# Reordering the local-attention stage of a two-branch block across tiles, with q's two rotary products split around ScalarE's square

## What is computed

```python
h = shift_token(x)                       # upper 64 channels come from the token before
q, k, v = split(h @ wqkv)                # 8 heads of 64
q, k = l2norm(q) * qs, l2norm(k) * ksc
q, k = rotary_xpos(q, k)                 # q * cos + rotate_half(q) * sin, the same for k
# windows of 64 queries see their own and the previous window of 64 keys
attn = softmax(mask(q @ k.T * 8)); o = attn @ v
x = x + o @ wo
h = layernorm(shift_token(x)); a, g = split(h @ w1 + b1)
x = x + (a * gelu(g)) @ w2 + b2
```

## Time and profile before

| | |
|---|---|
| median of 3 runs | 907.86 us |
| the profiled execution: its time, its span | 909.96 us, 908.2 us |
| PE busy | 800.1 us (88%) |
| DVE busy | 664.4 us (73%) |
| ACT busy | 654.3 us (72%) |
| POOL busy | 523.9 us (58%) |
| granted PE clock, mean | 0.972 of full |
| chain that ended last, by engine | PE 56%, ACT 17%, DVE 16%, issue 7% |

### The profile page before, as it was taken

How to read it: one execution, slowest core, us unless ns; L and a number is a source line. 1 busy time by engine, 2 the same in 40 slices (tenths; PEclk the granted TensorE clock), 3 DMA queues, 4 the chain that set the end, 5 groups by cost and what they waited for, 6 DMA issues and landing times.

```text
span 908.2 us, 26049 instructions
## 1 busy us (share of the span) xinstructions
PE 800.1 (88%) x9848; PEld 610.5 (67%) x9848; DVE 664.4 (73%) x1347; ACT 654.3 (72%) x2053; POOL 523.9 (58%) x521
## 2 busy tenths in 40 slices
PE   4779999779999999999989887999999999988985
PEld 1458778557777778777756545777877777775652
DVE  1577998677887787877457767778787788745765
ACT  2337777479899899889743337989988998974463
POOL 0363333078888888888511017888888888951100
PEclk8899999889999999999999998999999999999997
DMA  9110001012222222222201121222222222222001
GB/s 308 44 45 3 4 4 41 3 47 55 57 57 63 55 58 55 60 57 63 51 18 24 29 63 37 64 53 58 57 61 56 62 52 58 58 51 100 1 36 58
DMA packets 64704, 48.24 MB, mean 53 GB/s; under 512 B 40410, under 2 KB 50948, under 8 KB 64068
## 3 DMA queue, kind: packets, MB, share of 16 engines
q1 hardware_dynamic: 64580, 46.57, 19.9%
HBM read 10.63 MB, written 2.10 MB: 14 GB/s over the span
## 4 chain that ended last, share of the span: by engine, by line
PE 56%; ACT 17%; DVE 16%; issue 7%; POOL 1%; DMA 1%; SPq 1%; DVEq 0%; ACTq 0%; POOLq 0%
PE ps L415 47%; PE ps L425 9%; ACT prob L880 6%; DVE nmax L1130 3%; ACT sq L822 3%; DVE nt L1158 2%; ACT V L849 2%; ACT oT L831 2%; DVE split L970 2%; ACT kT L856 1%; ACT pT L826 1%; DVE prob L1217 1%; DVE split L968 1%; DMA awo<-in_awo 1%; ACT qT L841 1%
## 5 line engine op out<-in xcount | busy, mean ns | idle before, releaser
L880 ACT ACTIVATE prob<-ps,nmax 128x128 f32<-128x128 f32 x512 | 181.8, 374 | 36.7 <-DVE nmax L1130 36.7
L415 PE MATMUL ps<-wqkv,split 128*128 128x512 f32 x576 | 188.2, 438 | 14.2 <-DVE split L970 10.1
L1348 POOL TENSOR_TENSOR prob<-prob,rinv 128x512 f32<-128x512 f32 x128 | 133.9, 1046 | 88.4 <-DVE rinv L1116 45.8
L415 PEld LDWEIGHTS ps<-wqkv,split 128*128 128x128 f32 x576 | 97.5, 195 | 33.5 <-DVE split L970 10.2
L1130 DVE TENSOR_REDUCE nmax<-ps 128x4 f32<-128x512 f32 x128 | 83.6, 686 | 48.3 <-PE ps L415 48.3
L425 PE MATMUL ps<-ident,prob 128*128 128x128 f32 x640 | 98.3, 276 | 13.9 <-POOL prob L1348 13.1
L880 ACT ACTIVATION_READ_ACCUMULATOR prob<-ps,nmax 128x1 f32 x512 | 109.0, 213 | 0.0
L1359 POOL TENSOR_TENSOR qr<-qr,ss 128x512 f32<-128x512 f32 x64 | 66.9, 1046 | 53.7 <-DVE qr L1142 53.7
L425 PEld LDWEIGHTS ps<-ident,prob 128*128 128x128 f32 x640 | 76.2, 142 | 28.3 <-POOL prob L1348 17.4
L415 PE MATMUL ps<-oT,wo 128*128 128x128 f32 x512 | 73.9, 287 | 22.0 <-ACT oT L831 22.0
L826 ACT ACTIVATE pT<-ps 128x512 f32<-128x512 f32 x128 | 80.0, 625 | 10.7 <-PE ps L425 9.1
(11 more groups left out here) (139 smaller groups left out, 1871.9 us busy)
## 6 DMA issues: line engine op xcount, KB each, us to landing
VB<-V SPq DMA_DIRECT2D x129, 128.0 KB, 2.4
kT<-kT SPq DMA_DIRECT2D x65, 128.0 KB, 2.4
XS<-X SPq DMA_DIRECT2D x32, 128.0 KB, 2.3
XS<-X SPq DMA_DIRECT2D x128, 32.0 KB, 1.9
D<-in_xT SPq DMA_DIRECT2D x8, 256.0 KB, 4.4
XS<-in_xT SPq DMA_DIRECT2D x2, 1024.0 KB, 6.7
out_T<-XS SPq DMA_DIRECT2D x8, 256.0 KB, 2.0
raw<-in_wqkv SPq DMA_DIRECT2D x2, 768.0 KB, 4.4
```

The source lines that it names most:

```text
L415: return nc.tensor.matmul(o, l, r, start=start, stop=stop, skip_group_check=True)
L880: nc.scalar.activation(prob[:, par, grp, s * P:(s + 1) * P], ps[:, 4 + grp, s * P:(s + 1) * P], ACT.Exp, bias=nmax[:, par, grp * 4 + s:grp ...
L1348: g.tensor_tensor(p4, p4, rinv[:, slot, 4 * grp:4 * grp + 4].unsqueeze(2).broadcast_to([P, 4, P]), ALU.mult).then_inc(l_prob, 1)
```

## The change

The programs of all engines in the local stage are rewritten, with the same arithmetic but for these:

- The scaling of q by its norm on POOL (L1359) goes. The scores are now those of an unscaled q. DVE takes raw maxima (`rawmax`) and multiplies them by the norm in a small product (`scaled_maxima`), and ACT's exponentials get the norm as `scale`, read from `ss` for each partition, beside the `bias` that they had.
- The split of the input moves from DVE to POOL, in pieces of one tile (`input_high`, `input_low`).
- The copy of v moves from ACT to DVE (`v_copied`), and `V` and `ss` get a third buffer.
- For q, DVE makes the sine products first, ACT squares after them, and DVE makes the cosine product after the square.
- Semaphores that counted two groups or both q and k become one for each.
- The steps of a tile are spread over more steps n: q is projected 3 ahead (before 2), and the values of tile n-2 (before n-1) come right behind the scores of tile n and the transposes of q of tile n+1.

The new order on PE, on DVE and on ACT, as the diff has it, and SP's step:

```diff
+                def local(n, par):                    # PE
+                    q_projected(n + 3)
+                    k_turned(n)
+                    k_projected(n + 2)
+                    probs_turned(n - 2, 1)
+                    scores(n)
+                    q_turned(n + 1)
+                    values_summed(n - 2)
+                    probs_turned(n - 1, 0)
+                    output(n - 3)
+                    v_projected(n)
...
+                def values_summed(m):
+                    if 0 <= m < TILES:
...
+                        wait(pe, l_oe, base + m)
+                        pe.wait_ge(l_pTe[0], base + m + 1)
+                        pe.wait_ge(l_pTe[1], base + m + 1)
+                        pe.wait_ge(l_ve, base + m + 1)
+                        pe.wait_ge(v_prev[m % 2], 32 * ((base + m) // 2 + 1))
...
+                def local(n, par):                    # ACT
+                    q_squared(n + 3)
+                    norm_floor(n + 2)
+                    q_copied(n + 1)
+                    norm_log(n + 2)
+                    exponentials(n, 1)
+                    norm_inverse(n + 2)
+                    probs_copied(n - 1, 0)
+                    exponentials(n, 0)
+                    k_copied(n + 1)
+                    k_squared(n + 3)
+                    o_copied(n - 2)
+                    probs_copied(n - 1, 1)
...
+                    k_scaled(n + 1)                   # DVE
+                    q_rotated(n + 2)
+                    q_summed(n + 2)
+                    q_sin(n + 3)
+                    inverse_sums(n - 1, 0)
+                    v_copied(n - 1)
+                    k_summed(n + 2)
+                    maxima(n, 1)
+                    scaled_maxima(n, 1)
+                    inverse_sums(n - 1, 1)
+                    maxima(n, 0)
+                    q_cos(n + 3)
+                    scaled_maxima(n, 0)
+                    added_to_x(n - 3)
...
+                    normalised(n, 0)                  # POOL
+                    input_low(n + 5)
+                    input_high(n + 6)
+                    k_rotated(n + 2)
+                    normalised(n, 1)
+                    k_cos(n + 3)
+                    k_sin(n + 3)
```

```diff
                 def back(n, par):                     # SP
-                    nxt = 1 - par
-                    copied = held(xs_before_local(L) + 32 * (n - 2))
-                    if live(n, -3, TILES):
-                        sp.wait_ge(xs_dma, copied)
+                    nxt, done = 1 - par, base + n + 1
+                    if live(n, -5, TILES):
+                        sp.wait_ge(xs_dma, xs_before_local(L) + 32 * (n - 4))
                     if live(n, 0, TILES):
-                        sp.wait_ge(l_tre, turned)
-                        wait(sp, l_score, scored)
+                        sp.wait_ge(l_tk, done)
+                        wait(sp, l_score[1], done - 1)
                         sp.dma_start(kT[:, nxt, :, 0:WIN], kT[:, par, :, P:P + WIN]).then_inc(k_prev[nxt], 16)
                         sp.wait_ge(l_ve, done)
-                        sp.dma_start(VB[64:P, par, :], V[0:64, par, :]).then_inc(v_prev[par], 16)
-                        wait(sp, l_o, pv1)
-                        sp.dma_start(VB[0:64, nxt, :], V[64:P, par, :]).then_inc(v_prev[nxt], 16)
-                    if live(n, -2, TILES):
-                        copy_shifted(XS[1], n - 2, P, x_before_local(L) + n - 1)
+                        sp.dma_start(VB[64:P, par, :], V[0:64, done % 3, :]).then_inc(v_prev[par], 16)
+                        wait(sp, l_o, done - 1)
+                        sp.dma_start(VB[0:64, nxt, :], V[64:P, done % 3, :]).then_inc(v_prev[nxt], 16)
+                    if live(n, -4, TILES):
+                        copy_shifted(XS[1], n - 4, P, x_before_local(L) + n - 3)
```

At the end of a layer DVE now runs `local(TILES)` ahead of `ffn_weights`, and the rest of the tiles later:

```diff
                 local(TILES - 1, 1)
-                inverse_sums(TILES - 1, 1)
+                local(TILES, 0)
                 ffn_weights(L)
                 links(0, 1, NEWTON, 0, 2)
                 centre(nb, 2, shifted(XS[1], 2, CHUNK), 2)
                 ffn_bias(L)
-                add_to_x(TILES - 2)
+                local(TILES + 1, 1)
...
+                local(TILES + 2, 0)
                 links(2, 1, 6, 2)
                 scaled(0, tA)
```

More of the change, by code:

```diff
@@ new lines, in scores @@
+                def scores(m):
+                    if 0 <= m < TILES:
+                        if m == 0:
+                            if L == 0:
+                                pe.wait_ge(a_done, TILES)
+                            else:
+                                pe.wait_ge(ffn_hid, NPART * L * CHUNKS)
+                        pe.wait_ge(l_tq, base + m + 1)
+                        pe.wait_ge(l_tk, base + m + 1)
+                        pe.wait_ge(k_prev[m % 2], 16 * ((base + m) // 2 + 1))
+                        wait(pe, l_exp[0], 4 * (base + m))
+                        wait(pe, l_exp[1], 4 * (base + m))
+                        first, par = min(m % TPB, 1), m % 2
+                        half = [slice(64 * i, 64 * i + 64) for i in range(2)]
+                        for w, grp in ((0, 0), (1, 1), (1, 0), (0, 1)):
+                            kind = 1 if w else first
+                            mm(ps[half[w], 4 + grp, :], ident_bf[half[grp], half[grp]],
+                               lmask[half[grp], bass.ds(kind * CHUNK, CHUNK)], True, False)
+                        for s in range(4):
+                            for w, grp in ((0, 0), (1, 1), (1, 0), (0, 1)):
+                                last = mm(ps[half[w], 4 + grp, s * P:(s + 1) * P],
+                                          qT[half[grp], par, s, half[w]],
+                                          kT[half[grp], par, s, 64 * w:64 * w + P], False, True)
+                                if s == 3 and w != grp:
+                                    last.then_inc(l_score[grp], 1)
@@ new lines, in probs_turned, with output @@
+                def probs_turned(m, grp):
+                    if 0 <= m < TILES:
+                        pe.wait_ge(l_prob[grp], base + m + 1)
+                        wait(pe, l_pTe[1 - grp], base + m + grp)
+                        for s in range(4):
+                            last = turn(ps[:, 6, s * P:(s + 1) * P], prob[:, m % 2, grp, s * P:(s + 1) * P])
+                        last.then_inc(l_pT[grp], 1)
+                def output(m):
+                    if 0 <= m < TILES:
+                        if m == 0:
+                            pe.wait_ge(wo_in, 16 * (L + 1))
+                        pe.wait_ge(l_oe, base + m + 1)
+                        if 0 <= m + 4 < TILES:
+                            pe.wait_ge(l_tq, base + m + 4 + 1)
+                        elif 0 <= m + 3 < TILES:
+                            pe.wait_ge(l_tk, base + m + 3 + 1)
+                        elif 0 <= m - 1 < TILES:
+                            pe.wait_ge(x_new, x_before_local(L) + m - 1 + 1)
@@ L673, in layer @@
                 pe.wait_ge(l_qm, base + TILES)
+                pe.wait_ge(l_sqq, base + TILES)
                 pe.wait_ge(l_kn, base + TILES)
@@ L685, in layer @@
                 norm_bcast(0, 0, nb, 0)
-                local(TILES + 1, 1)
                 norm_bcast(1, 1, nb, 1)
@@ new lines, in exponentials @@
+                def exponentials(m, grp):
+                    if 0 <= m < TILES:
+                        act.wait_ge(l_max[grp], base + m + 1)
+                        for s in range(4):
+                            col = slice(grp * 4 + s, grp * 4 + s + 1)
+                            nc.scalar.activation(prob[:, m % 2, grp, s * P:(s + 1) * P],
+                                                 ps[:, 4 + grp, s * P:(s + 1) * P], ACT.Exp, bias=nmax[:, m % 2, col],
+                                                 scale=ss[:, (base + m) % 3, 2 * s + grp:2 * s + grp + 1],
+                                                 accum_out=rsum[:, m % 2, col]).then_inc(l_exp[grp], 1)
@@ L1378, in _ @@
+                steps(-6, TILES - 1 + 0, local)
+                pool.wait_ge(l_trq, base + TILES)
                 nb = L * CHUNKS
```

504 lines of the change are left out of this document (239 added, 265 removed).

## The result

The kernel after takes 963.45 us (median of 4 runs, 953.43 to 971.17), the kernel before 907.51 (907.1 to 908.72). The ratio is 1.0577, with a 95% interval from 1.0494 to 1.066: 5.8% slower. The forecast was 937, with a range from 917 to 957. The sign and the place were right, the size was not.

A forecast was written before the change was run, and what follows sets the result against it. PE, 7.61 us a tile, nearly bound the kernel before; in the new order a cycle through SP's copies would, at 8.6. 909.96 + 10.6 (local stages) + 17 (drains) + 1 (start) = 938.6, less 2.1: said 937, range 917 to 957.

The forecast's parts named there:

- The ring: Local stage: a cycle through PE's scores and values, SP's issues and the XS and kT landings sets the tile's period.
- Rival 4: Local stage: the ring is hidden, the period is the engines' 7.6 us, total 884; chance 0.10 with cases in between.
- The size of the ring: Local stage: 8.37 us bare plus 0.15 and 0.08 for late landings, 8.6 a turn; +5.3 us a layer.
- The median: Whole kernel: the median of the runs lies 2.1 us under the profiled execution, as before the change.
- The engines' floor: Local stage: the engines alone allow about 7.6 us a tile (PE 7.61, ACT 7.58), paid only in the first five intervals.
- The second operand: ACT's exponentials: a second per-partition operand costs 0.085 us each, 0.68 us a tile, covered by the ring.
- The drain: From each layer's last scores to its feed-forward matmuls: about 25.2 us against 16.9, taken as +8.5 a layer, 17 in all.
- Rival 2: Behind the last scores: the ring holds but the drain costs only +3 us a layer, total 925; chance 0.12.
- The start: Ahead of the first scores of both layers: short moves against an unchanged chain, +1 us in all, between -2 and +4.
- Rival 3: Local stage: kT landings stay as late as before, the ring is 8.95 us, total 955; chance 0.10.
- The forecast's cause, instruction packets: kT copies: 16 KB instruction packets sharing the DMA engines make landings late; about 1 in 8 hit, at 1.2 us each.

The follow-up runs named there:

- experiment 1: Kernel after, with SP's wait for the last XS copy's landing moved from ahead of the kT copy to ahead of the next XS copies: 897.46 us, ratio 0.9896.
- 2: Kernel after, with SP also waiting for the second VB copy's landing before it issues the XS copies: 1070.9 us, ratio 1.1798.
- 7: Kernel after, with SP's XS wait moved behind the kT copy, kT sent first and the VB copies one tile later: 885.96 us, ratio 0.9762.
- experiment 3: Kernel after, with the exponentials' per-partition scale replaced by the constant 0.001: 957.22 us, ratio 1.0532.
- experiment 6: Kernel after, with each layer's end reordered (on DVE, `ffn_weights` and the first `links` ahead of the last tiles' additions): 949.14 us, ratio 1.0466.
- 8: Kernel after, with the edits of experiment 6 and 7 together: 874.79 us, ratio 0.9642; repeated with the exponentials' scale constant: 860.2 us.
- experiment 5: Kernel after, with three useless PE matmuls a tile ahead of the kT wait: 966.59 us behind the waits for ACT's copies, 962.13 us ahead of them.

## Why the prediction was right, and where it was wrong

**The ring: right, and shown from both sides.** The order scores, values, SP, landing of X, landing of kT, scores bounds the period. The chain shows it link by link; taking its X landing out gives 66 us back (experiment 1), another landing makes it longer by just that (2), and SP's order without it lets the period fall to the engines' 7.42 (7). Rival 4, the hidden ring, is out: neither landing came sooner than its row of before.

**The size of the ring: the first step that failed.** The forecast was 8.6 us a turn, 8.37 bare and 0.23 for late landings; measured were 8.86, of which 8.6 are bare. Two terms made the bare ring too short. Q's transposes were taken at 0.44, their cost inside a run of PE work; ahead of the values they cost 0.59 (360.14 to 360.73 in the chain, and the median of the turns), 0.15 more. PE's release by a landing was taken at 0.05, as for SP; it takes 0.20 (358.66 to 358.86), and 0.02 for SP. On top, 0.25 a turn were late landings, late issues (the first XS issue took 1.04 us at 432.88, in place of 0.60) and two falls of the clock, each of the three some 4 us over the 52 turns; that is about what was added for landings alone, so this term came out right partly by luck. 52 turns at 0.26 are 13.5 us. The first five intervals gave 1.2 back, and layer 1's stage of before took 257.3 where I had used 256.3 twice; that leaves 11.3, against the 11.5 by which the two local stages exceed the forecast. Late kT landings did become rare as forecast, and for the sum it changed little: 4 of 52 were more than 0.3 us above the median.

**The median: the second step that failed.** I carried over that the median lies 2.1 us under the profiled execution. It lies 10.0 over it. Without that, the terms miss by 953.4 - 938.6 = 14.8 us, 11.5 of it in the local stages; with it, the miss is 26. In this kernel, whose PE waits each turn, the clock falls in some tiles and not in others, and the runs spread over 20 us, where before the timed ones spread over 1.6. It is partly chance how far the median went: the same kernel's second set of runs has its at 955.12 (experiment 4), inside the range, with the same turns (8.91 and 8.80 in the mean). Nothing in the trace of before could give that size, but a spread that grows with new idle time on PE was left out of the range.

**The engines' floor: right in size, with another engine in front.** Forecast was 7.6, from PE's unbroken 7.61 and ACT's 7.58. Measured is 7.42 with ACT full and PE at 7.37 (193.58 of 195.00). The 7.61 of PE's chain was thus no floor to a tenth, and the forecast's "no order of the same matmuls" under 7.6 does not hold: the same work of PE took 0.24 less in the new order, and the turn without ACT's operand takes 7.32. Why was not tried. PE's usual wait is therefore 1.2 us, where 0.8 to 1 was forecast.

**The second operand: right.** The exponentials went from 374 to 470 ns, +96, where the row's estimate was 85; taken out again in experiment 3, the operand is worth 88. The Trainium skill, "ScalarE: Activation LUTs", section "What ACT_TABLE_LOAD costs", gives about 93 ns for a pointer operand; by that page, as an estimate, eight of them cost 0.74 us a tile, and the trace agrees (8 x 0.096 = 0.77).

**The drain: right, a little small.** +9.3 a layer for 8.5. The wait before `ffn_weights` is there, at 13.9 for 12.4; the low clock on the way there, 1.55 us, had no term. From `ffn_weights` to the feed-forward matmuls it is 12.2 for 12.8 (the terms written down add up to 25.0, not 25.2). But experiment 6 shows that this path is not alone: with the wait gone, 7.5 of the 9.3 stay in its profiled execution, so another path, through PE's work on the last tiles, is nearly as long, and the forecast did not see that one. Rival 2 is out.

**The start:** +2.6 for +1, nearly all of it ahead of layer 1, within the -2 to +4 given.

**Rival 3** had the period right in effect, 8.95 for 8.86, and before the 2.1 us are taken off its terms give 956.8 for the profiled execution's 953.4. Its reason, that landings stay as late as before, is not what happened.

**What stays open.** Why a single turn loses the clock. Falls come behind PE's idling in kernels with the ring, and in the drains, that of experiment 6 included, and none was seen in the steady local stages of experiments 7 and 8 (1.00 from 205 to 400 us). In the kernel after, the two waits of 2.66 and 2.90 us lost the clock and one of 2.58 kept it, but in experiment 5 one of 1.91 lost it and one of 1.82 kept it, so the length of the last wait alone does not tell.

## What to carry to other kernels

When a change moves work across steps, write down for each in-order queue, DMA issuers included, what it waits for and who waits for what it sends next, and look for a cycle that advances one tile a turn: its length, not any engine's load, is then the period. Price its links where they will stand (a transpose ahead of a dependent, a landing that releases PE), not at what they cost in the middle of a full engine. Then put what the next tile's critical work needs first in the queue and the housekeeping behind it: here two moved pieces of SP's program took the same rewrite from 5.8% slower to 2.4% faster than before.

## What the runs showed of the hardware

- In a wait of PE of 2.66 us the granted clock fell to 0.50, to 1.2 GHz, and stayed low for about 7 us, with PE full for 6 of them; the turn there took 10.94 us instead of 8.6. The time of one program followed its mean clock over eight runs from 951 to 971 us.
- In the chain PE mostly starts 0.20 us after the landing that releases it (358.66 to 358.86), SP's next issue 0.02 us after (356.27 to 356.29).
- Long kT landings are not a fixed property of the copy: 15 of 32 took 3.0 us or more before, and in 4 of 52 turns of the kernel after it took over 0.3 us more than the median of 2.57 from issue to scores. The forecast's cause, instruction packets, was not tried, nor was another.
- A second per-partition operand costs an exponential of 128x128 88 to 110 ns (374 to 470, 470 to 382, 491 to 381), and 0.09 us from start to start.
